# A decoder kernel on one core: scores and value products of two units as one group, deeper buffers, other orders on four engines

## What is computed

```python
x = x + attn(layernorm(x))           # 8 heads, relative positions
x = x + cross_attn(ctx, layernorm(x))
x = x + ffn(layernorm(x))            # six layers, below
# ffn: for i in range(6):
#   x = attn_layer(shift_tokens(x), Wqkv[i], ...) + x   # 16 heads of 64, l2-normed q and k, rotary, windows of 32
#   x = ffn_layer(shift_tokens(x), ...) + x             # layer norm, W1 to 2 x 341, gelu gate, W2
```

## Time and profile before

| | |
|---|---|
| time, three runs | 4276.14 us median (4275.76 to 4276.42) |
| the profiled execution's own time | 4277.26 us |
| its span, first to last instruction | 4275.5 us |
| busy share of the span: PE, DVE, ACT, POOL | 93%, 82%, 78%, 72% |
| mean granted TensorE clock | 0.983 of full speed |

### The profile page before, as it was taken

The page is one execution under the profiler, slowest core; times in us unless marked ns, Lnnn a source line. Parts: engine busy times, 40 slices in busy tenths (PEclk is TensorE's granted clock), DMA queues, the critical chain, the costliest instruction groups (busy, mean ns, idle before and its releaser), DMA issues.

```text
span 4275.5 us, 102722 instructions
## 1 busy us (share of the span) xinstructions
PE 3981.7 (93%) x30384; PEld 3060.7 (72%) x30384; DVE 3521.6 (82%) x11903; ACT 3326.0 (78%) x11558; POOL 3080.2 (72%) x3387
## 2 busy tenths in 40 slices
PE   7888887899999999999999999999999999999997
PEld 5777776677777777777777777777777777777774
DVE  5676665788888888888888888888888888888884
ACT  1455554788888888888888888888888888888885
POOL 2333332788888888888888888888888888888883
PEclk9999998899999999999999999999999999999997
DMA  4222221000000000000000000000000000000000
GB/s 147 80 80 80 80 82 61 22 5 2 2 2 7 22 2 2 2 1 27 2 2 2 2 7 22 2 2 2 7 22 2 2 2 2 8 2 2 2 2 20
DMA packets 76222, 86.74 MB, mean 20 GB/s; under 512 B 13622, under 2 KB 69396, under 8 KB 74836
## 3 DMA queue, kind: packets, MB, share of 16 engines
q1 hardware_dynamic: 75732, 80.87, 5.9%
HBM read 45.33 MB, written 35.52 MB: 19 GB/s over the span
## 4 chain that ended last, share of the span: by engine, by line
PE 75%; ACT 13%; issue 4%; DVE 4%; POOL 3%; DMA 0%; SPq 0%; DVEq 0%; POOLq 0%; ACTq 0%; PEldq 0%
PE bank_pair L1081 10%; PE bank L1092 9%; PE bank L1099 9%; PE bank L1146 8%; PE bank L453 7%; PE bank L1112 6%; PE bank L454 6%; PE bank L455 6%; ACT p L1258 3%; PE bank L1138 3%; PE bank_pair L557 1%; ACT L1207 1%; POOL xn_lo L1411 1%; PE bank L551 1%; PE bank L533 1%
## 5 line engine op out<-in xcount | busy, mean ns | idle before, releaser
L1258 ACT ACTIVATE p<-p,mx 128x128 f32<-128x128 f32 x3072 | 1194.8, 396 | 26.0 <-DVE mx L1341 25.4
L1416 POOL TENSOR_TENSOR rot<-own_crossed 128x512 f32<-128x512 f32 x768 | 986.2, 1284 | 296.8 <-DVE ri L1329 275.2
L1420 POOL TENSOR_TENSOR p<-p,ri 128x512 f32<-128x512 f32 x768 | 801.7, 1044 | 96.9 <-DVE ri L1329 96.8
L1341 DVE CUSTOM_DVE_ANT_0 p<-bank_pair,band_f 128x128 f32<-128x128 f32 x3072 | 701.8, 284 | 143.4 <-issue 136.5
L1405 POOL TENSOR_TENSOR rot<-rot,rn 128x512 f32<-128x512 f32 x768 | 806.3, 1050 | 11.4 <-ACT rn L1229 11.4
L1081 PEld LDWEIGHTS bank_pair<-qkT 64*128 64x128 f32 x6144 | 402.3, 186 | 306.1 <-issue 290.7
L1258 ACT ACTIVATION_READ_ACCUMULATOR p<-p,mx 128x1 f32 x3072 | 596.9, 194 | 0.0
L1350 DVE TENSOR_REDUCE ss<-sq 128x8 f32<-128x512 f32 x768 | 523.7, 682 | 72.5 <-ACT sq L1290 64.6
L453 PE MATMUL bank<-wqkv_hi,xs_lo 128*128 128x512 f32 x1152 | 526.9, 457 | 48.3 <-ACT rstd L1244 37.1
L1234 ACT ACTIVATE oT<-bank 128x256 f32<-128x256 f32 x768 | 291.8, 380 | 345.3 <-PE bank L1092 340.9
L1355 DVE COPY pTl<-bank 128x512 f32<-128x512 f32 x768 | 525.1, 684 | 36.9 <-PE bank L1112 32.4
(11 more groups left out here) (198 smaller groups left out, 7421.8 us busy)
## 6 DMA issues: line engine op xcount, KB each, us to landing
pos_scratch<-pos_sb SPq DMA_DIRECT2D x32, 1020.0 KB, 4.4
sc<-pos_scratch SPq DMA_DIRECT2D x32, 512.0 KB, 4.0
wqkv_raw<-in_L_ffn_Wqkv SPq DMA_DIRECT2D x6, 1536.0 KB, 6.6
ctx_sb<-in_ctx SPq DMA_DIRECT2D x32, 128.0 KB, 3.5
wo<-in_L_ffn_Wo SPq DMA_DIRECT2D x6, 512.0 KB, 3.8
mrow<-in_mask_BxS_fk SPq DMA_DIRECT2D x1, 2048.0 KB, 7.8
x_all<-in_x SPq DMA_DIRECT2D x4, 512.0 KB, 8.8
out<-res SPq DMA_DIRECT2D x8, 256.0 KB, 2.3
```

The costliest lines, as they stand in the source:

```text
L1258: last = nc.scalar.activation(p[:, j, h, :], p[:, j, h, :], ACT.Exp, bias=mx[:, j, h:h + 1], scale=-1.0, accum_out=psums[:, j, h:h + 1])
L1416: nc.gpsimd.tensor_tensor(rot[:, (k - 6) % 4, :, :], own[:, (k - 6) % 4, :, :], crossed[:, (k - 6) % 4, :, :], ALU.add).then_inc(L["rot0"], 1)
L1420: nc.gpsimd.tensor_tensor(p[:, j, :, :], p[:, j, :, :], ri[:, j, :].unsqueeze(2).to_broadcast([128, G, T]), ALU.mult).then_inc(L["pn"], 1)
```

## The change

- S of two units is one group of 16 instructions, emitted in odd steps for units k - 11 and k - 10, over both full banks of `bank_pair`. One semaphore count stands for a pair.
- PV of two units is one group, emitted in odd steps for units k - 19 and k - 18 (it was unit k - 15 in step k), over the whole of bank 3. `y_ps` of Wo now lies in the same columns as `oT_ps`. ACT copies both units out in one instruction.
- Buffers are deeper: `qkT` 4 (2), `v_sb` 16 (8), `mx`, `p`, `psums`, `ri` 5 (4), `pTl` 4 (2).
- The stages stand in other steps: v projection unit k - 7 (k - 9), masking on DVE k - 11 (k - 10), exponential k - 12 (k - 10), reciprocal and POOL's scaling k - 13 (k - 12), T2 and its copy k - 15 (k - 13), residual addition k - 18 (k - 16), rotary addition k - 5 (k - 6), rotary scaling k - 7 (k - 8).
- Every engine's order within a step is new, and the feed-forward items stand in other steps.

The diff, cut to what decides the order (TensorE whole in its order, DVE in its order):

```diff
-        v_ps = ffn_ps = banks[2]
-        oT_ps, y_ps = banks[3][:, 0:2 * T], banks[3][:, 2 * T:3 * T]
-        s_ps = bank_pair[:, :, 0:2 * T]
+        v_ps = ffn_ps = banks[2]
+        oT_ps, y_ps = banks[3][:, :], banks[3][:, 0:T]
+        s_ps = bank_pair[:, :, :]
...
+                if on(18) and (k - 18) % 2 == 1:
+                    pe.wait_ge(L["pT"], n(18) + 1)
...
+                    for w in range(2):
+                        u = k - 18 - 1 + w
+                        for h in range(G):
...
+                            last = nc.tensor.matmul(oT_ps[rows, c * T:(c + 1) * T], v_sb[:, u % 16, h, :], pTl[:, u % 4, h, :], start=True, stop=True)
+                    last.then_inc(L["PV"], 1)
+                if on(7) and k % 2 == 1:
+                    if k == 1 and at.ffn_before():
+                        pe.wait_ge(L["z"], QUADS + at.F)
+                    elif at.ffn(3):
+                        pe.wait_ge(Fm["xcg"], at.F + 1)
+                    elif at.ffn(5):
+                        pe.wait_ge(Fm["rstd"], at.F + 1)
+                    elif at.ffn(9):
+                        pe.wait_ge(Fm["gate"], 3 * at.F + 2)
+                    elif at.ffn(11):
+                        pe.wait_ge(Fm["u"], 3 * at.F + 1)
+                    elif at.ffn(13):
+                        pe.wait_ge(Fm["u"], 3 * at.F + 3)
...
+                    split_product(v_ps[:, :], ...).then_inc(L["proj"], 1)
+                if at.ffn(8):
+                    pe.wait_ge(Fm["gate"], 3 * at.F + 1)
+                    gate(1)
+                if at.ffn(9):
+                    if at.values_at(9):
+                        pe.wait_ge(L["v"], at.P + 2)
...
+                    gate(2)
+                if on(10) and (k - 10) % 2 == 1:
+                    pe.wait_ge(L["qkT"], n(10) + 1)
+                    if at.again(10, 2):
+                        pe.wait_ge(L["mx"], n(10) - 1)
+                    for w in range(2):
+                        j = (k - 10 - 1 + w) % 4
...
+                    last.then_inc(L["S"], 1)
+                if at.ffn(7):
...
+                    gate(0)
+                if on(18) and (k - 18) % UB == UB - 1:
...
+                    pe.wait_ge(L["oT"], at.pair(18) + 1)
...                  # Wo
+                if at.ffn(4):          # var
+                if at.ffn(10):
+                    pe.wait_ge(Fm["gate"], 3 * at.F + 3)
+                    value(0)
+                if at.ffn(11):         # waits for L["v"], P + 3
+                    value(1)
+                if at.ffn(15):         # y
                 if on(9):              # T1, as before
+                if on(15):             # T2, was on(13)
                 if on(4):              # q and k projection, as before
+                if at.ffn(2):          # centre
+                if at.ffn(11):
+                    pe.wait_ge(Fm["u"], 3 * at.F + 2)
                     value(2)
```

More of the change, by code:

```diff
@@ L878, in build @@
         rot = sb("rot", [128, 4, 2 * G, DL])
[L879 to L885, removed]
+        qkT = sb("qkT", [128, 4, 4, T])
+        v_sb = sb("v_sb", [128, 16, G, DL])
+        mx = sb("mx", [128, 5, G])
+        p = sb("p", [128, 5, G, T])
+        psums = sb("psums", [128, 5, G])
+        ri = sb("ri", [128, 5, G])
+        pTl = sb("pTl", [128, 4, G, T])
         oT = sb("oT", [128, 8, 2 * T])
@@ L983, in values_at @@
             def values_at(self, k):
[L984 removed]
+                return not self.fixed or self.U + k - 7 < LAYERS * UNITS
             def two(self, d):
@@ new lines, in emit @@
+                if at.ffn(8):
[4 more added lines that the diff above has]
+                        pe.wait_ge(L["v"], at.P + 2)
+                    else:
+                        pe.wait_ge(Fm["gate"], 3 * at.F + 2)
+                    gate(2)
[5 more added lines that the diff above has]
+                        j = (k - 10 - 1 + w) % 4
+                        for h in range(G):
+                            r = slice(h % 2 * DL, h % 2 * DL + DL)
+                            c = 2 * w + h // 2
+                            last = nc.tensor.matmul(s_ps[:, h % 2, c * T:(c + 1) * T], qkT[r, j, h // 2, :], qkT[r, j, 2 + h // 2, :], start=True, stop=True)
+                    last.then_inc(L["S"], 1)
@@ L1073, in emit @@
                     nc.tensor.matmul(ffn_ps[:, :], mean_w[:, :], xsq[:, :], start=True, stop=True).then_inc(Fm["var"], 1)
[L1074 to L1093, removed]
+                if at.ffn(10):
+                    pe.wait_ge(Fm["gate"], 3 * at.F + 3)
+                    value(0)
+                if at.ffn(11):
+                    if at.values_at(11):
+                        pe.wait_ge(L["v"], at.P + 3)
+                    else:
+                        pe.wait_ge(Fm["u"], 3 * at.F + 1)
+                    value(1)
+                if at.ffn(15):
+                    if at.values_at(15):
+                        pe.wait_ge(L["v"], at.P + 5)
+                    else:
+                        pe.wait_ge(Fm["u"], 3 * at.F + 3)
+                    pe.wait_ge(Fm["w2_in"], 32 * (at.lf + 1))
+                    pe.wait_ge(Fm["u"], 3 * at.F + 3)
+                    for c, (c0, m) in enumerate(FF_CHUNKS):
+                        last = nc.tensor.matmul(ffn_ps[:, :], w2[0:m, c, :], uf[0:m, c, :], start=(c == 0), stop=(c == 2))
+                    last.then_inc(Fm["y_mm"], 1)
                 if on(9):
@@ L1123, in emit @@
                                   [w[:, 0:2, g * G * DL:(g + 1) * G * DL] for w in wqkv]).then_inc(L["proj_qk"], 1)
[L1124 to L1147, removed]
@@ L1380, in emit @@
                     last.then_inc(L["z"], 1)
+                if on(18) and (k - 18) % UB == UB - 1:
+                    dve.wait_ge(L["WO"], at.batch(18) + 1)
+                    for rows, kept in kept_halves(at.own_batch(18), 1):
+                        zb = kept.rearrange("p a n -> p (a n)")
+                        last = nc.vector.tensor_tensor(zb, y_ps[rows, :], zb, ALU.add)
+                    last.then_inc(L["res"], 1)
+                if at.ffn(9):
+                    keep_gate(2)
+                if on(13):
+                    dve.wait_ge(L["exp"], n(13) + 1)
+                    nc.vector.reciprocal(ri[:, n(13) % 5, :], psums[:, n(13) % 5, :]).then_inc(L["ri"], 1)
                 if at.layer_start(1) and k == 15:
```

301 lines of the change are left out of this document (131 added, 170 removed).

## The result

The changed kernel takes 4521.34 us (median of four, 4519.90 to 4525.86) against 4275.95 us before (4275.37 to 4276.42): 1.0576 times as long, 95% interval 1.0557 to 1.0594. The forecast was 4417 us and a range of 4290 to 4475. The direction was right; the size was not, +245 us instead of +141, and the time lies outside the range.

The account below looks back on a forecast made before the run. TensorE bounds the kernel; a body goes from 71.63 to 74.6 us, grouping's 2.8 saving included, new waits 8.8 where 2.5 stood. 46 x 3.0 = 138, some 3 at the end: 4417 us, range 4290 to 4475.

Parts of the forecast that it names:

- What bounds it: Middle of the six layers: TensorE sets the pace at 96.4% busy, DVE close behind at 88%; TensorE about 89% afterwards.
- What grouping saves: S and PV on TensorE: one group for two units saves 0.35 us per pair, 2.8 per body, 134 in all.
- Rival (c): S and PV: a second unit costs nearer to a new group, up to 129 us more; chance 0.06 together with (d).
- The prediction's other estimate: TensorE's mode changes, priced by the documented drain of 53 ns: two fewer per pair save 41 us instead of 134.
- What else changes: Fewer ACT copies of `oT`, deeper buffers, same DVE and POOL instructions: worth nothing, 0 to 10 us either way.
- Rival (d): POOL falls behind and T1 waits some tenths per pair, 115 us more; chance 0.06 together with (c).
- The new waits: TensorE's uneven steps wait for DVE and ACT: 8.8 us per body where 2.5 stood, body 74.6 us; chance 0.69.
- windows 1, 7, 11, 13 and 15: Stretches from end of S in odd step k to that in k + 2: 10.15, 10.7, 9.8, 8.2, 8.85 us.
- windows 5 and 9: Stretches from S of steps 5 and 9: 8.2 us with Wo's wait on ACT, 10.9 with v's wait on `value(0)`.
- The first two bodies, without feed-forward: First two of 48 bodies: steps in pairs at about 6.26 us, or 7.8 with waits; net change nothing.
- (a): TensorE sets the pace throughout and the whole saving of 134 us comes through, 4143 us; chance 0.12.
- (b): The chains of waits hold, but fewer or shorter: 4259 us, or 4345 if more of them bind; chance 0.13.

Follow-up runs that it names:

- the split: Kernel with the grouping alone in the old order, its groups issued as S, PV, S, PV of one unit each: 4303.01 us, 1.0063 to the kernel before.

## Why the prediction was right or wrong

**What bounds it.** Right as far as before goes: TensorE paced it, and its share afterwards is 89%, as forecast. DVE's share fell further than said, to 484.85 / 600 = 81% and not 85%, as the body is longer.

**What grouping saves.** Right: 0.35 us a pair, by the slots of the changed kernel and by the split. Rival (c), a dearer second unit, is out. The Trainium skill (TensorEngine Tiling (Array Packing), Key Properties) says that changing the tiling mode drains the array; the trace agrees that two such changes less are worth something, 0.35 us here. The prediction's other estimate, 41 us or 0.11 a pair, was too low; the measurement decides.

**What else changes.** Right: the deeper buffers are worth nothing. Rival (d) is out: all that TensorE waits for POOL in those 2400 us of the changed kernel is 1.6 us.

**The new waits.** The waits through `keep_gate(0)`, the copy of v, `value(1)`, `xcg` and `pTl` were there, at the forecast's size: windows 1, 7, 11, 13 and 15 are 0.0 to 0.1 off. Those of windows 7 and 11 were taken away one at a time, and these windows fell by 1.44 and 1.11. The step that failed is the reading of windows 5 and 9. "Wo now waits in its own step for ACT's two copies after v, 0.15 beyond S: windows 5 and 13 at 8.2", and "v and S, 0.1 unhidden: 1.97, so 10.9" let S start as soon as v ends. They came out at 8.79 and 11.83. I had used the copy `qkT` for ACT's own order in window 1, and not asked in each window when ACT gets to it: S of step k needs the unit that T1 transposed in step k - 1. In steps 6 and 10 ACT does `xn` and the gelus first. Taking that away gave 0.49 and 0.84 us a body, 61 us of the 104 by which the forecast was low.

The rest is in small terms. The masking came 0.26 us after S's slot (3109.33 - 3107.98 - 1.09) instead of 0.2, T2 0.15 after the end of the copy's work, modelled, instead of 0.1, and T2 with its projection took 1.26 (3114.06 - 3112.80) instead of 1.14. So window 3 was 0.21 short, and the other six misses of 0.1 and less add 0.53: 0.74 x 46 = 34 us. That is 95 us of the 98 by which the 46 bodies were low (235.8 instead of 138). "The first two bodies, without feed-forward" at nothing was right within 2 us: the windows there are 8.01 and 8.3, and from T1 of step 17 to that of step 31 the changed kernel takes 57.0 us against 54.5, but it had been 3.2 ahead. "Some 3 at its end" for the two deeper steps was 8.7. 61 + 34 + 6 - 2 = 99 of 104.

The range failed with the step. Its 46 us were for handoffs of 0.1; a whole wait that one has not listed is 23 to 66 us in this kernel (0.49 to 1.44 us a window, 46 times).

**The rivals.** (a) and (b) were wrong for this order. The thought of (a), that TensorE's saving comes through, is only partly true even in the old order: 58 us of 134. The low clock accounts for some of the other 76. In the trace of the kernel with the grouping alone, the stretches at 1.2 GHz after 780 us add up to 130 us, with the groups split to 72; at half speed that is up to (130 - 72) / 2 = 29 us. The rest is some 47 us. Most of it went into waits that stand in both kernels and are longer with the groups merged: from 1500 to 3900 us TensorE waits 69.2 us for POOL's `xn_lo` and 29.4 for ACT's copy `oT`, against 56.3 and 17.8 with the groups split; the sum of all its waits is 155 against 132, an estimated 33 us over the six layers (23 x 3400 / 2400).

**What stays open.** Of the 276 us between the new orders and the old one with the same groups, edits of single waits gave back 153 (to 4368 us). The other 123 are not assigned one by one. Part is in windows without feed-forward work: 8.0 us without Wo and 8.3 with it, where the old order with the same groups takes 6.4 and 8.05 in its first bodies. Three more edits, on either kernel, only shifted the loss. A better order than 4243 us was not found.

## What to carry to other kernels

A saving on the engine that sets the pace counts only as far as the order around it stays even: merge two units' work, and everyone who waits for the second waits for both. When forecasting such an order, go through every semaphore that the instruction at the end of each window waits for, in each window, and ask when its producer's list gets there; one forgotten wait (0.42 and 0.78 us here) outweighs several handoffs of 0.1. And gains of moved waits don't add up: 143 us for three edits one at a time, 128 for the three and two more together. A table of medians hides the few bodies that are unlike the rest; add up the whole span as well.

## What the hardware showed that was not expected

In the kernel with the grouping alone, TensorE idled for 1.76 us ahead of gate 0, did three products, and then S of 16 instructions took 2.00 us and PV 1.70 instead of 1.09 and 1.03, at a granted clock of 0.50, where it had been 1.00 before and was again afterwards. The wait stands in every body, the slow S doesn't: of 46 windows behind it 27 last 6.8 us, 14 last 8.4, and five, at the start of a layer, 10.0 or more. Where it happens, 1.6 us come on top of a wait of 1.8, so a short idle stretch on the pacing engine can cost nearly twice itself. What decides between the 27 and the 14 the runs don't show; the wait is as long in both. The changed kernel idles more, yet its stretches at the low level after 780 us add up to 65 us, against 56 before and 130 with the grouping alone; why its waits leave the clock alone wasn't found out. With gate 0 and value 1 moved, where S waits 1.7 and 1.9 us a body instead, they add up to 159.
